# Queries and keys of a first attention projected once, and their threefold rows made by DMA through DRAM

## The reference, cut to what matters

```python
q = _heads(x @ Wq + bq)            # 16 heads of 8; x is layer-normalised
k = _heads(x @ Wk + bk)
att = jnp.einsum('bhqd,bhkd->bhqk', q, k) * scale     # causal mask, softmax, times v
qc = _heads(x @ Wcq + bcq)
kc = _heads(cross_input @ Wck + bck)
attc = jnp.einsum('bhqd,bhkd->bhqk', qc, kc) * scale  # softmax, times vc
```

## Time and profile before

| | |
|---|---|
| runs | 1323.44, 1322.62, 1314.83 us |
| profiled execution | 1322.67 us, its span 1320.9 us |
| granted TensorE clock, mean | 0.847 of full speed |
| PE busy | 1137.6 us (86%) |
| DVE busy, ACT busy | 706.6 us (53%), 494.1 us (37%) |
| DMA moved | 56.85 MB, mean 43 GB/s |

### The profile page before, as it was taken

One profiled execution on the slowest core, in us unless ns is written; L12 is line 12 of the kernel. 1 busy time (PEld: TensorE's weight loads), 2 busy tenths in 40 slices (PEclk: granted clock), 3 DMA queues, 4 the chain that ended last, 5 costly groups with the idle time before them and its releaser, 6 DMA issues.

```text
span 1320.9 us, 21222 instructions
## 1 busy us (share of the span) xinstructions
PE 1137.6 (86%) x8499; PEld 883.2 (67%) x8499; DVE 706.6 (53%) x1867; ACT 494.1 (37%) x1022; POOL 85.0 (6%) x134
## 2 busy tenths in 40 slices
PE   6888779989989988989988988988998998985696
PEld 4547545777668765877577855976577766874475
DVE  5514466646565557547665658546664656423500
ACT  4233415352534425451634334442535253422120
POOL 0010002000110002000200011000200011000000
PEclk8558959899789979998889978998889978977556
DMA  7000000242020420142022221042023210133222
GB/s 212 0 1 4 3 0 1 48 69 65 8 49 17 69 55 21 29 76 57 6 49 47 47 47 46 5 77 63 1 48 67 64 40 13 29 56 84 52 44 52
DMA packets 198032, 56.85 MB, mean 43 GB/s; under 512 B 173568, under 2 KB 193838, under 8 KB 197934
## 3 DMA queue, kind: packets, MB, share of 16 engines
q1 hardware_dynamic: 195630, 51.20, 19.9%
q10 hardware_dynamic: 2304, 4.29, 1.1%
HBM read 31.36 MB, written 24.12 MB: 42 GB/s over the span
## 4 chain that ended last, share of the span: by engine, by line
PE 75%; DVE 11%; ACT 7%; issue 3%; SPq 3%; DMA 2%; ACTq 0%; DVEq 0%
PE bank L928 10%; PE bank L737 10%; PE bank L773 9%; PE bank L884 5%; PE bank L663 5%; PE bank L843 4%; PE bank L624 3%; PE bank L678 3%; PE bank L588 3%; DVE negmax L1261 3%; ACT pa L1022 3%; PE bank L942 2%; PE bank L860 2%; PE bank L688 2%; PE bank L911 2%
## 5 line engine op out<-in xcount | busy, mean ns | idle before, releaser
L1022 ACT ACTIVATE pa<-bank 128x512 f32<-128x512 f32 x224 | 123.4, 596 | 122.8 <-PE bank L678 75.8
L1261 DVE TENSOR_REDUCE negmax<-bank 128x2 f32<-128x512 f32 (+1 forms) x224 | 139.0, 683 | 41.9 <-PE bank L526 22.1
L1039 ACT ACTIVATE pa<-bank,b_c 128x256 f32<-128x256 f32 x256 | 107.5, 471 | 128.6 <-PE bank L737 127.3
L928 PE MATMUL bank<-vb,pb 128*128 128x65 f32 x1024 | 137.1, 299 | 4.2 <-issue 4.2
L928 PEld LDWEIGHTS bank<-vb,pb 128*128 128x128 f32 x1024 | 132.8, 214 | 10.3 <-issue 7.9
L737 PE MATMUL bank<-xnT_a,w 128*128 128x256 f32 x512 | 138.1, 417 | 0.1
L773 PE MATMUL bank<-w,pa 128*128 128x128 f32 x1024 | 124.2, 276 | 0.0
L773 PEld LDWEIGHTS bank<-w,pa 128*128 128x128 f32 x1024 | 121.9, 192 | 3.2
L1101 ACT ACTIVATE pb<-bank 128x512 f32<-128x512 f32 x128 | 69.9, 602 | 125.4 <-PE bank L888 125.4
L737 PEld LDWEIGHTS bank<-xnT_a,w 128*128 128x128 f32 x512 | 101.1, 208 | 17.3 <-ACT pa L1039 0.5
L1415 DVE TENSOR_REDUCE negc<-bank 128x2 f32<-128x512 f32 x128 | 80.0, 684 | 58.8 <-PE bank L860 58.6
(11 more groups left out here) (240 smaller groups left out, 1706.3 us busy)
## 6 DMA issues: line engine op xcount, KB each, us to landing
v_d<-at SPq DMA_DIRECT2D x32, 256.0 KB, 3.3
vb<-v_d SPq DMA_DIRECT2D x32, 256.0 KB, 6.0
at_d<-at SPq DMA_DIRECT2D x32, 256.0 KB, 2.1
at<-at_d SPq DMA_DIRECT2D x32, 256.0 KB, 4.4
pv_d<-pvs SPq DMA_DIRECT2D x8, 512.0 KB, 3.1
pvs<-pv_d SPq DMA_DIRECT2D x16, 256.0 KB, 4.2
w<-in_L_ffn_W_dram ACTq DMA_DIRECT2D x1, 2048.0 KB, 11.5
bd<-mix_d SPq DMA_DIRECT2D x128, 8.0 KB
```

Source lines behind the costliest of these rows:

```text
L928: mm = pe.matmul(BB[2 + qt][:, i * (DH + 1):(i + 1) * (DH + 1)], pb[:, h % NPB, kt * T + qt * P:kt * T + (qt + 1) * P], vb[:, kt, h, :], s ...
L1022: nc.scalar.activation(pa[:, e % NPA, :], BA[e % 2][:, :], ACT.Exp, scale=SC0).then_inc(S["a_ex"], 1)
L1039: ins = nc.scalar.activation(hT[:, u % 4, c, :], BA[u % 2][:, c * T:(c + 1) * T], ACT.Relu, bias=b1_c[:, k:k + 1])
L1261: nc.vector.tensor_reduce(negmax[:, i:i + ng], BA[j][:, :].rearrange("p (g k) -> p g k", g=ng), AX, ALU.max, negate=True).then_inc(S["a_mx ...
```

## The change

`f_stack` becomes `f_heads(half)`: four matmuls for a sequence instead of 16, one for each kind, with the 128 columns of the weight in the order (d, h). ACT adds the bias and rounds to the high part (four instructions instead of 16), DVE subtracts to give `lo_part` (four instead of 16). SP then copies the parts out to two DRAM tensors, `q_d` with 25 rows and `k_d` with 24, in which the high part stands twice and the low part once, and eight DMAs (step `f_spread`) read them back into the strips of `qs` and `ks`: for each of the four strips 25 rows of q and 24 of k, every row in four pieces of 2 KB. `a_max(0)` waits for those eight. At the start `qs` and `ks` are blanked by DVE and a row of zeros goes to `q_d`; `w_stack`, `lo_c`, `lo_bias` and what made them are gone. The orders of steps are new lists.

```diff
-        w_stack = sb("w_stack", [P, 4, G, P])
+        w_heads = sb("w_heads", [P, 4, P])
+        lo_part = sb("lo_part", [P, 4, T], F32R)
+        qs_all = sb("qs", [P, G, 2, T], F32R)
+        ks_all = sb("ks", [P, G, 2, T], F32R)
+        ROWS = 3 * D + 1
+        q_d = dram("q_d", [ROWS, H, 2, T])
+        k_d = dram("k_d", [ROWS, H, 2, T])
...
+        STEPS_A = [("a_values", 0), *run("a_max", 0, 7), ("a_shift", 0), *run("a_score", 0, 14), ("a_lastpv", 0),
+                   ("a_heads", 0), ("a_project", 0), ("a_norm2", 0), ("c_kv", 0), ("a_norm2_apply", 0),
+                   ("a_router", 0), ("f_load", 0), ("a_expert", 0), ("a_expert", 1), ("f_norm", 0),
+                   *run("a_expert", 2, 8), ("f_norm_apply", 0), ("a_last", 0), ("c_norm", 0), ("c_norm_apply", 0),
+                   ("f_heads", 0), ("c_q", 0), ("f_heads", 1), ("c_max", 0), ("c_turn", 0), ("c_out", 0),
+                   ("f_spread", 0)]
+        AFTER_A = (49, 61, 62, 63, 63, 65, 65, 67, 68, 69, 70, 73, 73, 75, 79, 81, 81, 82, 82, 84, 84, 85, 85, 86,
+                   87, 87, 88, 90, 91, 92, 96, 98, 99, 100, 101, 102, 103, 104, 105, 108, 108, 109, 110)
...
+        LAST_B = [("b_norm", 0), ("b_norm_apply", 0), ("b_gates", 0), ("b_split", 0), ("b_top2", 0),
+                   ("b_split", 1), ("b_top2", 1), ("b_top2", 2), *run("b_split", 2, 5), ("b_fill", 0),
...
+            order += [("f_heads", 0, 0), ("f_heads", 1, 0), ("f_spread", 0, 0), ("s_rows", 0, 0), ("s_bias", 0, 0)]
...
+                    def s_cols(_):
+                        sp.wait_ge(s_blank, 2)
+                        for sc in range(2):
+                            sp.dma_start(q_d[3 * D, :, sc], qs[0:H, 0, 0, :].bitcast(F32)).then_inc(s_zero_row, 16)
+
+                    def f_heads(half):
+                        for u in (2 * half, 2 * half + 1):
+                            rows_d, kind = (k_d if u % 2 else q_d)[:, :, u // 2], KINDS[u]
+                            first = 0 if u % 2 else D
+                            sp.wait_ge(S["a_mh"], upto("a_mh", u + 1))
+                            sp.dma_start(rows_d[first:first + 2 * D].rearrange("(r d) h n -> (d h) r n", d=D),
+                                         hi_part[:, kind, :].unsqueeze(1).broadcast_to([P, 2, T])).then_inc(S["f_hw"], 16)
+                            rest = 2 * D - 2 * first
+                            sp.wait_ge(S["a_split"], upto("a_split", u + 1))
+                            sp.dma_start(rows_d[rest:rest + D].rearrange("d h n -> (d h) n"), lo_part[:, kind, :].bitcast(F32))\
+                                .then_inc(S["f_lw"], 16)
+
+                    def f_spread(_):
+                        sp.wait_ge(S["f_hw"], upto("f_hw", 64))
+                        sp.wait_ge(S["f_lw"], upto("f_lw", 64))
+                        if now[0] == 0:
+                            sp.wait_ge(s_zero_row, 32)
+                        else:
+                            sp.wait_ge(S["a_st"], upto("a_st", 0))
+                        for j in range(4):
+                            for stack, rows_d, n in ((qs_all, q_d, ROWS), (ks_all, k_d, ROWS - 1)):
+                                sp.dma_start(stack[32 * j:32 * j + n, :, :, :].rearrange("p g s n -> p g (s n)").bitcast(F32),
+                                             rows_d[0:n].rearrange("r (g j) s n -> j r g (s n)", j=4)[j]).then_inc(S["f_st"], 16)
...
-                    def f_stack(u):
-                        kind = KINDS[u // 2]
-                        if u == 0:
+                    def f_heads(half):
+                        if half == 0:
                             pe.wait_ge(S["f_xc"], upto("f_xc", 1))
...
                         for c in range(2):
-                            g = 2 * (u % 2) + c
+                            kind = KINDS[2 * half + c]
                             rows, rhs = (CC, cxT_a) if kind == KC else (P, xnT_f)
-                            mm = pe.matmul(BA[2 + u % 2][:, c * T:(c + 1) * T], w_stack[0:rows, kind, g, :], rhs[:, :],
+                            mm = pe.matmul(BA[2 + half][:, c * T:(c + 1) * T], w_heads[0:rows, kind, :], rhs[:, :],
                                            start=True, stop=True)
...
                         if m == 0:
-                            pe.wait_ge(S["a_split"], upto("a_split", 16))
+                            pe.wait_ge(S["f_st"], upto("f_st", 128))
+                            pe.wait_ge(S["a_split"], upto("a_split", 4))
                             pe.wait_ge(S["a_vc"], upto("a_vc", 1))
...
+                    def f_heads(half):
+                        act.wait_ge(S["a_pj"], upto("a_pj", half + 1))
+                        for u in (2 * half, 2 * half + 1):
+                            kind = KINDS[u]
+                            nc.scalar.activation(hi_part[:, kind, :].bitcast(F32R), BA[2 + half][:, (u % 2) * T:(u % 2 + 1) * T],
+                                                 ACT.Identity, bias=bias_c[:, kind:kind + 1]).then_inc(S["a_mh"], 1)
...
+                    def f_heads(half):
+                        dve.wait_ge(S["a_mh"], upto("a_mh", 2 * half + 2))
+                        for u in (2 * half, 2 * half + 1):
+                            kind = KINDS[u]
+                            nc.vector.scalar_tensor_tensor(lo_part[:, kind, :], BA[2 + half][:, (u % 2) * T:(u % 2 + 1) * T],
+                                                           bias_c[:, kind:kind + 1], hi_part[:, kind, :],
+                                                           ALU.add, ALU.subtract).then_inc(S["a_split"], 1)
```

More of the change, by code:

```diff
@@ L352, in run @@
             return [(name, i) for i in range(first, end)]
-        STEPS_A = [("a_values", 0), *run("a_max", 0, 7), ("a_shift", 0), ("a_score", 0), ("a_score", 1),
-                   ("f_load", 0), *run("a_score", 2, 14), ("a_lastpv", 0), ("a_heads", 0), ("a_project", 0),
-                   ("c_kv", 0), ("a_norm2", 0), ("a_norm2_apply", 0), ("a_router", 0), *run("a_expert", 0, 3),
-                   ("f_norm", 0), *run("a_expert", 3, 8), ("f_norm_apply", 0), ("a_last", 0), ("c_norm", 0),
-                   *run("f_stack", 0, 4), ("c_norm_apply", 0), ("c_q", 0), ("f_stack", 4), ("c_max", 0),
-                   ("f_stack", 5), ("f_stack", 6), ("c_turn", 0), ("c_out", 0), ("f_stack", 7)]
@@ new lines, in transformer_program @@
+        STEPS_B = [("b_norm", 0), ("b_norm_apply", 0), ("b_gates", 0), ("b_split", 0), ("b_split", 1),
+                   ("b_top2", 0), ("b_split", 2), ("b_top2", 1), ("b_top2", 2), *run("b_split", 3, 8),
+                   *run("b_max", 0, 7), ("b_fill", 0), ("b_max", 7), ("b_shift", 0), ("b_mix", 0), ("b_score", 0),
+                   ("b_mix", 1), ("b_score", 1), ("b_sel", 0), ("b_score", 2), ("b_score", 3), ("b_attend", 0),
+                   ("b_score", 4), ("b_score", 5), ("b_attend", 1), ("b_score", 6), ("b_score", 7),
+                   ("b_attend", 2), ("b_attend", 3), ("b_gather", 0), ("b_weigh", 0), ("b_gather", 1),
+                   ("b_out", 0)]
@@ L507, in b_out @@
                             sp.wait_ge(S["a_out"], upto("a_out", 16))
-                    own = dict(f_load=f_load, s_first=s_first, b_gates=b_gates, b_split=b_split, b_top2=b_top2, b_fill=b_fill, b_mix=b_mix, b_sel=b_sel,
+                    own = dict(f_load=f_load, s_first=s_first, s_cols=s_cols, f_heads=f_heads, f_spread=f_spread, b_gates=b_gates, b_split=b_split, b_top2=b_top2, b_fill=b_fill, b_mix=b_mix, b_sel=b_sel,
                                b_attend=b_attend, b_weigh=b_weigh, b_out=b_out)
```

143 lines of the change are left out of this document (41 added, 102 removed).

## The result

The changed kernel takes 1414.49 us (median of four runs, 1409.97 to 1424.25) against 1323.03 us: the ratio is 1.0726, with the interval 1.0683 to 1.0769. The forecast was 1300 us, in a range of 1275 to 1326. It was slower, and by more than the slow rival said. The profiled execution has a span of 1409.0 us, 88.1 more than before.

A forecast was written before the change was run, and what follows sets the result against it. PE, busy 86% of the span, was taken as the bound. Start +15.9, first boundary +1.4, periods -51.6, stalls +13.2 and end -2.0 gave -23.1 us: from 1322.67 to 1300 us, range 1275 to 1326.

The forecast's parts named there:

- the slow rival: PE's wait at a_max(0) replaces the saved work, with half clock costing some 2 us a period: 1338 us, chance 0.10.
- The work taken off PE: Each period: 6.4 us of matmuls and 3.1 of gaps gained, 0.9 lost at a_max, 8.6 us before the new wait.
- the start of f_spread: On SP, behind b_attend(0): transfers start 5.8 us after PE's end of f_heads(1).
- PE's arrival at a_max(0): PE needs the gathered data 15.3 us behind f_heads(1), 0.7 us of it for hand-overs.
- T: Time from SP's first issue of f_spread to its last DMA's landing: forecast 11.7 us, with 7.4 and 13.4 kept.
- T - 9.5: PE's stall at a_max(0) in a period: T up to 9.5 us is hidden; 2.2 us forecast.
- The start and first boundary: First sequence loses T + 4.2, 15.9 us; the first boundary loses T - 10.3, 1.4 us.
- The end: Last b stream: b_top2 no longer waits behind the splits on DVE, 2 us gained.
- the rival I gave 0.25: Few engines share the gathers, five for 25 rows and twelve for 24: T = 13.4, 1313 us, chance 0.25.
- my sum: Whole change in time: 8T - 116.7 us for T of 9.5 or more, -23.1 us with T = 11.7.
- the lost cover: Between a_max(0) and a_max(1) one b_score of 1.14 us replaces a b_attend of 3.72: 0.9 us charged a period.

The follow-up runs named there:

- e12: Changed kernel with seven 4 KB transfers, one after the other, in place of the eight gathers: 1364.25 us, 1.0315 of the kernel before.
- e1: Changed kernel without the eight gathers, a_max(0) waiting only for the writes to q_d and k_d: 1269.22 us, 0.9601 of the kernel before.
- e8: Kernel before, with only its order of stream b around a_max made that of the changed kernel: 1363.62 us, 1.0305.
- e7: Changed kernel with 20 useless 128x256 matmuls on PE ahead of the wait for the gathers: 1390.12 us, 1.053 of the kernel before.

## Why the prediction was wrong

**Right.** The work taken off PE: 8.3 us a period by the kernel without gathers, 8.6 forecast. Its terms were less exact than their sum: in the five full periods from sequence 2 on, PE's busy time shrank by 7.3 us and its idle time by 1.6, where I had 6.4 and 2.2. Nearly right were the start of f_spread, 6.2 us behind PE's end of f_heads(1) on average, where I had worked out 5.8, and PE's arrival at a_max(0), 14.3 us behind it, for 15.3. Together they make the stall 1.4 us longer for the same T: 7.6 us a period on average, where T - 9.5 gives 6.2. The start and first boundary, with the measured T in my own formula: (15.7 + 4.2) + (15.7 - 10.3) = 25.3 us, measured 26.9. The end (from the first a_max of sequence 7 on) is 3.3 us longer and not 2 shorter. In the kernel without gathers it takes 283.1 us against 288.8 before, 5.7 less, so what follows the last wait costs 9 us there as well.

**Wrong, the term T.** I took 11.7 us, from the 2 MB load, and held 13.4 for the upper end. It is 15.7. Three sizes failed. An issue of such a gather takes SP 0.74 or 0.77 us (medians), not 0.32 as the 8 KB copies of the earlier trace rows: the last of the eight is issued 5.7 us after the first. And few engines share them: the DMA share is 0.72 and 0.73 while gathers of both kinds run, 12 of 16 engines, and falls behind the last issue to 0.34 and 0.32, 5 engines, at 108 GB/s. That is the rival I gave 0.25, "five for 25 rows, twelve for 24", with its mechanism, and it gave T = 13.4. By the rule of the Trainium skill ("DMA: Bandwidth & Descriptors", section "Why a DMA increments its semaphore by 16 and not by 1") the traces agree: 5 engines work for 25 rows, and 12 while gathers of 24 rows run too. The third size is the packet. My argument against that rival, that packets alone may be quicker than 101 ns, holds for the end (5.1 engines at 108 GB/s are 97 ns for 2 KB), but from 644 to 646 us 11.5 engines moved 138 GB/s, which is 171 ns, and in the next two 11.7 moved 185, 129 ns. How the difference between 13.4 and 15.7 is shared between issues and packets wasn't tried. With T = 15.7 my sum gives 8 x 15.7 - 116.7 = +8.9 us, 1332.

**Wrong, and worse: the price of the half clock behind the wait.** The measured difference is +88, so 79 us are missing, and 73 of them are in the six periods: my formula says -8.6 + (15.7 - 9.5) = -2.4 us each, and they grew by 9.7. The forecast's sum charged a stall with its own length (T - 9.5) and the half clock behind it with nothing, though its stall of 2.2 us was longer than the gap of 2.10 us behind which the earlier trace rows show 0.50; only the slow rival had 2 us a period for it. This step would have failed with T = 11.7 too: in e12 waits of 2.2 to 3.0 us cost 8.6 us a period beyond their length. Set against the kernel without gathers, with the same 1032 to 1033 instructions, a period of after from one a_max(0) to 0.3 us ahead of the next reads

```profile
655.20:811.00 155.80, 138.77 (x1032) 108.27 (x1032) 81.87 (x218) 54.23 (x113) 9.84 (x14) 0.81 0.28 60
```

155.8 - 136.5 = 19.3 us longer, 14.6 of it busy time (138.77 - 124.17) and 4.7 idle. It is one of the longer periods. All six, from the first a_max of sequence 1 to that of sequence 7, in the changed kernel and then without gathers:

```profile
190.18:1116.92 926.74, 810.81 (x6018) 628.02 (x6018) 488.12 (x1298) 322.56 (x674) 56.88 (x83) 0.82 0.27 59
```

```profile
163.41:982.62 819.21, 742.57 (x6019) 577.37 (x6019) 486.70 (x1298) 320.68 (x672) 56.36 (x83) 0.91 0.26 55
```

That is 17.9 us a period longer, 11.4 busy and 6.5 idle. The stall of 7.6 us is partly paid back by gaps that close: those of 0.25, 0.22 and 0.9 us that the kernel without gathers has behind a_max(0) are gone. The same matmuls at the slower clock cost 11.4 us, more than five times the rival's figure. That is the mechanism of my slow rival (stall and half clock at a_max(0)), given 0.10 and 1338 us; both of its sizes were too small.

**The wait and the order.** A wait of 2 to 3 us alone brings 31 us at half clock a period. The order alone costs the kernel before 40 us, but that the lost cover, which I had priced at 0.9 us, cost the changed kernel anything isn't shown: without gathers the same order kept its clock in all six periods, and with the wait left in place the cover brought next to nothing back. Without a wait, it turned 24 to 27 us at half clock into 17. I compared the orders step by step for what DVE would be late with, and never for what PE would be doing while its clock was at stake: behind the earlier trace rows I read a low clock as an effect of a gap just there, with an end of its own, and not as a state that outlasts its cause by 20 to 30 us.

**What stays open.** Why, with the same matmuls at the same distances and no wait, one period keeps its clock and the next loses it. It isn't the gathers, for the kernel before in the new order has none and shows both kinds; whether they shift the odds these runs can't tell: without gathers 7 of 12 periods without a wait kept the clock (all six of e1, one of e8's), with fast gathers in this order 2 of the 6 with a wait of 0.03 us or less, and none of the 14 with 0.07 to 0.77 us. Whether so short a wait decides it wasn't tried.

## What to carry to other kernels

Before a transfer is put between a producer and the busiest engine, work out how many engines its outer dimension lets share it, and which partitions it lands on: 25 rows in a strip cost 15.7 us, the same bytes over all partitions 8.7. Price a wait of the busiest engine by its length and by the clock it loses afterwards, which here was the larger part. A change of order can cost clock with no wait and no transfer added; try it alone on the old kernel, where here it cost 40 us, and on the new one without its transfers, which kept the forecast gain.

## What the hardware showed

- The granted clock fell behind a wait of 2.2 us as surely as behind one of 7.5, and the stretch at 0.50 (the level of 1.2 GHz) then lasted 31 and 34 to 37.5 us (from within the wait on, in the longer case), through b_attends that kept PE busy at 28.8 of 30 us. Useless matmuls that filled the wait completely didn't hold it: 24 to 27 us at 0.50 in all six steady periods (e7).
- 32 neighbouring partitions: 16 busy engines moved 197 to 222 GB/s; partitions four apart over all 128: up to 291 GB/s in the stretch shown. By the Trainium skill, page "SBUF — State Buffer", section "Door 1: The DMA port swizzle (why `[64,N]` ≈ `[32,N]`)", a block of 32 neighbouring partitions reaches half of the 16 ports; the runs agree. The rows' order in DRAM changed with the partitions and wasn't tried alone.
- While 12 engines worked on gathers of 25 and 24 rows, 2 KB took one engine 129 to 171 ns (185 and 138 GB/s in all), with 5 engines 97 ns (108 GB/s).
- An issue by SP took 0.74 us for a gather of 25 rows and 0.77 for one of 24 (medians), 0.60 with 32 rows or with the blocks, and 0.32 for the 8 KB copies.
